# Second attention of a four-part layer stack on Trainium2: per-head turns and projections issued in halves over separate slots

## What is computed

```python
# 16 sequences of 64 tokens, 256 wide, 32 heads of 8 in the reference's own function;
# the input here has 8 sequences of 256 tokens
q, k, v = [(x @ w.T).reshape(B, S, 32, 8).transpose(0, 2, 1, 3) for w in (wq, wk, wv)]
scores = jnp.einsum('bhqd,bhkd->bhqk', q, k) / jnp.sqrt(8.0) + bias(rel_pos, S)
attn = jax.nn.softmax(scores, axis=-1)
ctx = jnp.einsum('bhqk,bhkd->bhqd', attn, v).transpose(0, 2, 1, 3).reshape(B, S, 256)
y = ctx @ wo.T
```

## Time and profile before

| | us |
|---|---|
| median of 3 runs | 997.85 |
| lowest, highest | 994.13, 998.16 |
| the profiled execution, its own time | 999.12 |
| its span in the profile | 997.1 |
| PE, ACT, DVE busy over the span | 882.9, 693.2, 704.8 |

### The profile page before, as it was taken

How to read it: one execution, slowest core, us unless ns; L and a number is a source line. 1 busy time by engine, 2 the same in 40 slices (tenths; PEclk the granted TensorE clock), 3 DMA queues, 4 the chain that set the end, 5 groups by cost and what they waited for, 6 DMA issues and landing times.

```text
span 997.1 us, 21097 instructions
## 1 busy us (share of the span) xinstructions
PE 882.9 (89%) x7200; PEld 719.8 (72%) x7200; DVE 704.8 (71%) x2130; ACT 693.2 (70%) x1538; POOL 260.6 (26%) x360
## 2 busy tenths in 40 slices
PE   4778899999899988888989898989888999899995
PEld 3556788888788975666666666666665888789884
DVE  6877788888855567778787778787777562365437
ACT  2878766867765358988888888888888322366646
POOL 0345622333432202002020102010100347334432
PEclk9989999999999989999999999999999999999997
DMA  6203022010000102011111111101020312244434
GB/s 191 65 1 107 5 72 86 12 33 23 22 23 23 43 12 65 2 26 42 26 40 27 38 30 33 34 10 46 9 62 23 101 55 94 70 112 113 113 129 183
DMA packets 54761, 54.87 MB, mean 55 GB/s; under 512 B 17953, under 2 KB 48929, under 8 KB 54658
## 3 DMA queue, kind: packets, MB, share of 16 engines
q1 hardware_dynamic: 51250, 44.18, 15.1%
q0 software_dynamic: 3408, 9.34, 2.8%
HBM read 32.85 MB, written 20.65 MB: 54 GB/s over the span
## 4 chain that ended last, share of the span: by engine, by line
PE 53%; DVE 18%; ACT 16%; issue 8%; DMA 2%; POOL 1%; another core or an unknown queue 1%; DVEq 0%; ACTq 0%; SPq 0%; POOLq 0%
PE ps L445 11%; PE ps L447 10%; PE ps L446 10%; PE ps L968 5%; PE ps L985 4%; ACT G L1487 4%; PE ps L676 3%; PE ps L956 3%; ACT wu_rows L1487 3%; ACT G L1497 2%; DVE G L2032 2%; PE ps L749 2%; PE ps L1154 1%; ACT RT L1247 1%; DVE wu_rows L2032 1%
## 5 line engine op out<-in xcount | busy, mean ns | idle before, releaser
L1487 ACT ACTIVATE G<-G,small 128x256 f32<-128x256 f32 x296 | 133.3, 511 | 25.2 <-DVE small L2032 25.0
L2032 DVE CUSTOM_DVE_ANT_0 G<-ps,nb 128x256 f32<-128x256 f32 x296 | 111.2, 420 | 44.1 <-PE ps L956 43.7
L445 PE MATMUL ps<-WU 128*128 128x256 f32 x384 | 117.0, 305 | 17.1 <-DVE wu_rows L1854 6.9
L1497 ACT COPY G<-ps 128x512 f32<-128x512 f32 x192 | 112.1, 584 | 13.9 <-PE ps L968 13.5
L2393 POOL TENSOR_SCALAR_AFFINE_SELECT G<-G 128x256 f32<-128x256 f32 x128 | 76.4, 620 | 146.5 <-ACT G L1332 146.3
L446 PE MATMUL ps<-WU 128*128 128x256 f32 x384 | 108.4, 282 | 0.0
L447 PE MATMUL ps<-WU 128*128 128x256 f32 x384 | 108.3, 282 | 0.0
L1487 ACT ACTIVATE wu_rows<-wu_rows,small 128x256 f32<-128x256 f32 x216 | 97.7, 510 | 15.2 <-DVE small L2032 14.9
L2032 DVE CUSTOM_DVE_ANT_0 wu_rows<-ps,nb 128x256 f32<-128x256 f32 x216 | 81.3, 420 | 32.4 <-PE ps L956 32.1
L968 PE MATMUL ps<-ident,G 128*128 128x128 f32 x592 | 91.8, 283 | 13.3 <-DVE G L2042 9.5
L2360 POOL TENSOR_SCALAR small<-small 128x2 f32<-128x2 f32 x16 | 7.0, 440 | 324.6 <-DVE small L1678 324.6
(11 more groups left out here) (251 smaller groups left out, 2374.4 us busy)
## 6 DMA issues: line engine op xcount, KB each, us to landing
xs<-G SPq DMA_DIRECT2D x8, 645.0 KB, 6.7
G<-xs SPq DMA_DIRECT2D x39, 128.0 KB
G<-x SPq DMA_DIRECT2D x17, 256.0 KB, 2.9
G<-in_x SPq DMA_DIRECT2D x16, 256.0 KB, 2.9
wu_rows<-yy SPq DMA_DIRECT2D x8, 512.0 KB, 6.9
x<-G SPq DMA_DIRECT2D x15, 256.0 KB, 2.2
wu_rows<-in_wu SPq DMA_DIRECT2D x8, 384.0 KB, 5.1
wraw<-in_wu SPq DMA_DIRECT2D x8, 256.0 KB, 3.0
```

The costliest lines, as they stand in the source:

```text
L445: pe.matmul(o, lh, rh, start=start, stop=False, skip_group_check=True)
L1487: m = act.activation(p, p, ACT.Exp, scale=-1.0, bias=mneg[:, k:k + 1])
L1497: act.copy(probT(h), halves(2 + h % 2)).then_inc(probT_act, 1)
L2032: m = dve.tensor_tensor_reduce(prob(H2 * i + h)[:, t, :], ps[:, SCORE_BANKS[h % 3], S * t:S * (t + 1)], nbv[:, t, :], 1.0, -FMIN, ALU.add, ...
```

## The change

The work stays the same, instruction for instruction, in the second attention; only the slots change. On TensorE the turns of q's heads and of k's heads get slots of their own (q at 26, 28, 0, 3; k at 27, 30, 2, 4, where both were at 26, 30, 2, 4), `x_turn` goes in two halves at 6 and 7, each tile's q and k product in two halves of three matmuls at 9 and 10, 15 and 16, and `ct_turn` in halves at 17 and 18. The wait for `v_staged` goes from the first q turn to the k turns. ScalarE's copies of q's heads go to 27, 29, 1, 4 (from 27, 31, 3, 5), `x_hi` to 7 (6), `context_hi` to 19 (18), `hi_parts` to 11 and 17 (10 and 16). VectorE's copies of k's heads go to 28, 31, 3, 5 (27, 31, 3, 5), `context_lo` to 20 (19), and the low parts, for q and for k apart, to 12, 13 and 18, 18 (12 and 18, both in one). The diff:

```diff
@@ -75,11 +75,11 @@
 
 
 
-PE2 = dict(heads=(26, 30, 2, 4), x_turn=6, qk=(9, 15), c_turn=(8, 10, 12, 14), ct_turn=17, v=20,
-           project=22)
-ACT2 = dict(heads=(27, 31, 3, 5), place_v=7, x_hi=6, context_hi=18, hi_parts=(10, 16), stage_v=21)
-DVE2 = dict(heads=(27, 31, 3, 5), outputs=(14, 22, 30, 6), x_lo=8, context=(9, 11, 13, 15),
-            context_lo=19, add=24, norm=26, lo_parts=(12, 18))
+PE2 = dict(q_heads=(26, 28, 0, 3), k_heads=(27, 30, 2, 4), x_turn=(6, 7), qk=(9, 10, 15, 16), c_turn=(8, 10, 12, 14),
+           ct_turn=(17, 18), v=20, project=22)
+ACT2 = dict(heads=(27, 29, 1, 4), place_v=7, x_hi=7, context_hi=19, hi_parts=(11, 17), stage_v=21)
+DVE2 = dict(heads=(28, 31, 3, 5), outputs=(14, 22, 30, 6), x_lo=8, context=(9, 11, 13, 15),
+            context_lo=20, add=24, norm=26, lo_parts=(12, 13, 18, 18))
 TURN_LAG = 4
 
 ACT_TAKES_EVEN = (0, 4)
@@ -633,22 +633,24 @@
         def _(pe):
             pe.wait_ge(ident_ready, 2)
 
-            def x_turn(f, b):
+            def x_turn(f, b, parts=range(KT)):
 
                 pe.wait_ge(xt_loaded[f], 16 * b + 16)
-                for k in range(KT):
+                for k in parts:
                     for t in range(2):
                         m = pe.transpose(ps[:, B_XT[f], S * k + P * t:S * k + P * (t + 1)],
                                          xt_in_a[:, t, P * k:P * (k + 1)], ident[:])
-                m.then_inc(xt_turned[f], 1)
-
-            def qk(f, b, t):
+                if KT - 1 in parts:
+                    m.then_inc(xt_turned[f], 1)
+
+            def qk(f, b, t, parts=range(KT)):
 
                 tok = slice(P * t, P * (t + 1))
-                for k in range(KT):
+                for k in parts:
                     m = product3(pe, ps[:, b_qk(f, b, t), :], XT_a[0][:, k, tok], XT_a[1][:, k, tok],
                                  AW[:, 0, k, 0:512], AW[:, 1, k, 0:512], k == 0, k == KT - 1)
-                m.then_inc(qk_ready[f], 1)
+                if KT - 1 in parts:
+                    m.then_inc(qk_ready[f], 1)
 
             def v(f, b):
 
@@ -664,9 +666,10 @@
                 pe.wait_ge(heads_q[f], 4 * b + n)
                 pe.wait_ge(heads_k[f], 4 * b + n)
 
-            def heads(f, b, n):
-
-                for src, bank, out in ((QS, B_QT[f], heads_q[f]), (KS, B_KT[f], heads_k[f])):
+            def heads(f, b, n, parts=range(2)):
+
+                for part in parts:
+                    src, bank, out = ((QS, B_QT[f], heads_q[f]), (KS, B_KT[f], heads_k[f]))[part]
                     w = src.bitcast(F32).rearrange("p (t g c) -> p t g c", t=2, g=8)
                     if n:
 
@@ -691,14 +694,15 @@
                     m = pe.transpose(ps[:, LAST_C[n] if last else C_BANKS[f][n], P * g:P * (g + 1)], ot[:, 4 * c + g, P * t:P * (t + 1)], ident[:])
                 m.then_inc(c_turned[f], 1)
 
-            def ct_turn(f, b, last=False):
+            def ct_turn(f, b, last=False, parts=range(KT)):
 
                 pe.wait_ge(ctx_done[f], len(C_BANKS[f]) * (b + 1))
-                for k in range(KT):
+                for k in parts:
                     for t in range(2):
                         m = pe.transpose(ps[:, LAST_CT if last else B_CT[f], S * k + P * t:S * k + P * (t + 1)],
                                          ctx_a[:, t, P * k:P * (k + 1)], ident[:])
-                m.then_inc(ct_turned[f], 1)
+                if KT - 1 in parts:
+                    m.then_inc(ct_turned[f], 1)
 
             def project(f, b, last=False):
 
@@ -996,37 +1000,40 @@
                             turn(i, h - TURN_LAG, first)
                         if h % 4 == 1 and (h >= 9 or not first):
                             mix(i if h >= 9 else i - 1, (h - 9) // 4 % 8, first)
-                        if h in PE2["heads"][2:]:
-                            heads(2, i, 2 + PE2["heads"][2:].index(h))
-                        if h == PE2["x_turn"]:
+                        if h in PE2["q_heads"][2:]:
+                            heads(2, i, 2 + PE2["q_heads"][2:].index(h), (0,))
+                        if h in PE2["k_heads"][2:]:
+                            heads(2, i, 2 + PE2["k_heads"][2:].index(h), (1,))
+                        if h == PE2["x_turn"][0]:
                             heads_out(2, i, 4)
-                            if left:
-                                x_turn(2, i + 1)
-                        if h == PE2["qk"][0] and left:
-                            pe.wait_ge(xt_ready[2], i + 2)
-                            qk(2, i + 1, 0)
+                        if h in PE2["x_turn"] and left:
+                            x_turn(2, i + 1, (PE2["x_turn"].index(h),))
                         if h in PE2["c_turn"] and not first:
                             c_turn(2, i - 1, PE2["c_turn"].index(h), 8)
-                        if h == PE2["qk"][1] and left:
-
-                            pe.wait_ge(split_ready[2], 4 * (i + 1) + 2)
-                            qk(2, i + 1, 1)
-                        if h == PE2["ct_turn"] and not first:
-                            ct_turn(2, i - 1)
+                        if h in PE2["qk"] and left:
+                            t, k = divmod(PE2["qk"].index(h), KT)
+                            if t == 0:
+                                pe.wait_ge(xt_ready[2], i + 2)
+                            else:
+                                pe.wait_ge(split_ready[2], 4 * (i + 1) + 2)
+                            qk(2, i + 1, t, (k,))
+                        if h in PE2["ct_turn"] and not first:
+                            ct_turn(2, i - 1, False, (PE2["ct_turn"].index(h),))
                         if h == PE2["v"] and left:
 
                             pe.wait_ge(split_ready[2], 4 * (i + 1) + 4)
                             v(2, i + 1)
                         if h == PE2["project"] and not first:
                             project(2, i - 1)
-                        if h == PE2["heads"][0] and left:
-
-                            pe.wait_ge(v_staged[2], i + 2)
+                        if h in PE2["q_heads"][:2] and left:
+
                             if not first:
                                 pe.wait_ge(out_step[2], OUT_STEPS[2] * (i - 1) + 5)
-                            heads(2, i + 1, 0)
-                        if h == PE2["heads"][1] and left:
-                            heads(2, i + 1, 1)
+                            heads(2, i + 1, PE2["q_heads"].index(h), (0,))
+                        if h in PE2["k_heads"][:2] and left:
+
+                            pe.wait_ge(v_staged[2], i + 2)
+                            heads(2, i + 1, PE2["k_heads"].index(h), (1,))
 
                 passes(n, one)
 
@@ -1708,16 +1715,21 @@
                 dve.wait_ge(ct_hi[f], b + 1)
                 dve.tensor_tensor(CT_a[1], halves(LAST_CT if last else B_CT[f]), CT_a[0].bitcast(F32), ALU.subtract).then_inc(ct_ready[f], 1)
 
-            def qk_lo_parts(b, t):
+            def qk_lo_part(b, t, w):
                 src = ps[:, b_qk(2, b, t), :].rearrange("p (w h d) -> p w h d", w=2, h=H2)
                 dve.wait_ge(split_hi[2], 8 * b + 4 * t + 4)
-                for w, (dst, places) in enumerate(((QS, (1, 3)), (KS, (2, 3)))):
-                    d5 = dst.rearrange("p (t h s d) -> p t h s d", t=2, h=H2, s=4)
-                    for s in places:
-                        m = dve.scalar_tensor_tensor(out=d5[:, t, :, s, :], in0=src[:, w],
-                                                     scalar=QSCALE if w == 0 else 1.0,
-                                                     in1=d5[:, t, :, 0, :].bitcast(F32), op0=ALU.mult, op1=ALU.subtract)
-                m.then_inc(split_ready[2], 2)
+                dst, places = ((QS, (1, 3)), (KS, (2, 3)))[w]
+                d5 = dst.rearrange("p (t h s d) -> p t h s d", t=2, h=H2, s=4)
+                for s in places:
+                    m = dve.scalar_tensor_tensor(out=d5[:, t, :, s, :], in0=src[:, w],
+                                                 scalar=QSCALE if w == 0 else 1.0,
+                                                 in1=d5[:, t, :, 0, :].bitcast(F32), op0=ALU.mult, op1=ALU.subtract)
+                m.then_inc(split_ready[2], 1)
+
+            def qk_lo_parts(b, t):
+
+                for w in range(2):
+                    qk_lo_part(b, t, w)
 
             def k_heads(b, n):
                 dve.wait_ge(heads_turned[2], 8 * b + 2 * n + 2)
@@ -2082,8 +2094,9 @@
                             if h == DVE2["norm"]:
                                 norm(2, i - 1, 2, xr_a, xo_a)
                         if left:
-                            if h in DVE2["lo_parts"]:
-                                qk_lo_parts(i + 1, DVE2["lo_parts"].index(h))
+                            for part, at in enumerate(DVE2["lo_parts"]):
+                                if h == at:
+                                    qk_lo_part(i + 1, part // 2, part % 2)
                             if h in DVE2["heads"][:2]:
```

## The result

The changed kernel takes 1012.1 us (median of 4 runs, 1011.3 to 1014.8) against 997.3 us before (4 runs, 994.1 to 998.2): a ratio of 1.016, 95% interval 1.0138 to 1.0181. It is slower by 14.8 us. Forecast were 1009 us, and the time lies inside the range of 993 to 1016. The profiled execution had 1011.25 us with a span of 1009.2.

A forecast was written before the change was run, and what follows sets the result against it. No engine is full; waits between in-order engines bound the pass, by how many slots they reach. Six passes at 1.55, 1.0 for the first and 1.06 for the last add 11.4 us: forecast 1009 us, range 993 to 1016.

The forecast's parts named there:

- Part 1: Turns of q's heads, slots 26 to 4: turn at 28 waits, scores 30 come 2.0 us late, scores 6 1.06 late.
- Part 2: x's turn and first qk half, slots 6 to 10: x_lo's wait hidden by the mix, scores 10 0.27 us late.
- Parts 3 and 4: Slots 11 to 20: VectorE waits for ScalarE's high parts before low parts; row-minimum 14 1.4, slot 20's turn 1.55 us late.
- The sum: Whole kernel: 1.55 us for six passes, 1.0 for the first, 1.06 for the last, 11.4 us longer.
- Rival (a), the clock: TensorE's clock falls in all seven passes, not four; slot 20's wait grows over 1 us: 1014 us, chance 0.15.
- Rival (b), faster: Second attention: scores 10, 16 and 18 come earlier, new waits not met, about 1.5 us a pass gained: 987 us, chance 0.16.

## Why the prediction was right, point by point

The mechanism was right but for the cover of x's low part, and the time was close; the cost of a full pass was put at about two thirds of what it is.

- **What bounds the kernel.** Right: no engine full, a wait's reach in slots decides. ScalarE's busy time in a pass is 44 to 45 us in all runs while the pass went from 48.7 to 52.6.
- **Part 1.** Right in mechanism and size. Forecast: turn of q at slot 28 behind 1.4 of idle time, scores 30 and scores 0 2.0 late, the pass 1.06 late after slot 6. Measured: 1.47; scores 30 to scores 0 of the next pass as forecast (680.39 and 683.91, against 565.55 and 569.08 after shifting by the 112.75 between scores 28 of both traces, are 2.1 late); 1.18 alone.
- **Part 2.** Right sign, term too small: scores 10 forecast 0.27 late. By the time from `place_v` to scores 10 (3.25 before, 2.76 after the earlier trace rows) and a `place_v` that came 1.17 late, they were 0.68 late. Three things were off: Part 1 left 1.17 and not 1.06; the first half of a qk product takes 0.90 and not 0.80 (645.80 to 646.70; the second half, with a turn behind it, takes 0.77); and x's low part isn't hidden by the mix but holds the product back another 0.2. The run with x halved shows the last by itself (0.2 a pass).
- **Parts 3 and 4.** Right mechanism: VectorE waits for ScalarE ahead of both groups of low parts, forecast about 1 in slot 12 (1.13) and near 1 in slot 18 (0.60, smaller), and slot 20's turn late behind them. Forecast 1.28 from slot 10 to 20, measured 2.25 - 0.68 = 1.57. The waits were costed by start to start of the high parts (1.05 for four); a consumer on another engine starts only after the last row's end (660.47 + 1.19 = 661.66, VectorE at 661.69), 0.17 later in each of the two places, which is about the 0.29 that is missing.
- **The sum.** Terms too small, total near by luck. 1.55 a pass forecast, 2.25 measured; the 0.7 that was missing is in the two items above. All that the sum counts lies within the seven windows from the first `place_v` to the last, since the Part 1 of the last pass ends the seventh of them. There 11.4 were forecast and 15.3 measured. The first window (48.23 to 50.15) is 1.9 longer, where the terms for the first pass and for one Part 1 make 2.06, so what was short is six full passes at 0.7. The time still came out at 14.8 for a forecast of 12 from the same median. In the profiled executions the stretch up to the first `place_v` was 1.1 shorter, and that from the last one to the end 2.1 (258.5 for 260.6); neither was forecast, and both may be chance between executions.
- **Rival (a), the clock.** It didn't take place in the changed kernel (four passes with a fall before and after, though one fall is now at slot 28; the wait at slot 20 grew by 0.75 and not by over 1), but falls were more in the runs with one part of the change alone (six, six and seven), where they hid in part what the edit did. The Trainium skill's "TensorE: Matmul & The Clock Gate", section "HAM oscillation — how this bites in real kernels", says that idle gaps between bursts of matmuls bring the low clock; it speaks of longer gaps than any here, and these traces show falls at waits of 1.2 to 2.9 us. The ends of the series agree with the rule: the run whose waits were 0.20 and 0.67 had no fall, the one with 2.44 at slot 20 had one in every pass. Between them length doesn't decide: the changed kernel and the one without its turns have the same 2.08 at slot 20, and the clock fell there in three passes of the first and in six of the second. The section's advice to do all K tiles together is given for loops that wait between them. Here other work of TensorE lies between the halves, and the halved products made the pass shorter by 0.6 with as many falls as before.
- **Rival (b), faster.** Its point of decision was right: less than 0.3 us of idle time of VectorE ahead of the low parts. With the parts put back that time is nil, and the kernel is as fast as before (0.9987, 0.9968 to 1.0005) though TensorE still waits 1.47 in slot 28.

## What to carry to other kernels

When work is moved between slots of a loop that runs on several in-order engines, count for each wait how many slots lie between the producer's place and the consumer's, and compare that with how far the consumer runs ahead of the producer. Here an edit that spread work evenly but took such a distance from three slots to one (or from two to one) lost 1.0 to 1.7 us a pass, and the burst had cost 0.6. Split the work and keep the distances: with the products and the turns of heads split and two slots kept the kernel was 1.15% faster than before, and 1.5% with v's product moved along, not 1.6% slower. And look at the clock of each pass before comparing times of two variants.

## What the runs showed of the hardware

One fall of TensorE's clock to its lower level costs this loop 1.5 us at slot 20 and 1.2 to 1.4 at slot 28, and whether it comes depends on more than the length of the wait ahead: with a wait of 1.30 to 1.33 us at slot 20 it fell in four of six passes in the kernel before, and in none of the last five in the run with the parts put back; with 2.56 in the first pass of the changed kernel it didn't fall. Otherwise equal passes of one execution differ in this, so single edits of 1.0 to 1.2 us a pass (0.7 to 0.8% of the kernel) were partly masked: three runs with full passes of 51.3 to 51.6 (one of them estimated) had medians of 1008 to 1014, and one with 50.83 had 996. In the changed kernel one of the four falls came right behind the new wait of slot 28, in a pass of 53.75 us, and the mix there took nearly twice its 1.00:

```profile
624.65 0.63 PE L679 MATMUL ps<-ident,RT 128*128 128x128 f32 x4 [1.47 <-ACT RT L1254]
625.11 0.63 PE L972 MATMUL ps<-ident,wu_rows 128*128 128x128 f32 x4
625.68 1.94 PE L989 MATMUL ps<-G 128*32 128x256 f32 x16
```

(TensorE's timeline of the changed kernel.) Why a given pass is hit stays open. Also open is why the spread of the runs is that wide for some kernels (999.8 to 1013.4 for the changed one without its turns): a trace was read for one execution of each only.
